# Router logits from extra columns, paired half-height products in the experts' first layer, and a GELU wait per chunk

## Chip, cores and metric

The kernel runs on one core of a Trainium2 chip. The metric is the device time of the program in microseconds (us). The engines are TensorE (PE in the profile; its weight loads are PEld), VectorE (DVE), ScalarE (ACT), GpSimd (POOL) and SyncE (SP, which here only issues DMAs).

## What is computed

The reference is one layer of a language-model tower on 32 sequences of 128 tokens with 192 features. Shortened to what matters here:

```python
emb  = word_table[ids] + domain_table[dom] @ proj_w.T + proj_b + types + pos
x    = layernorm(emb) * gamma + beta
x    = x + magnitude_attention(x)              # 12 heads of 16
x1   = plain_layernorm(x)                      # input of the transformer block
h    = x1 + causal_attention(ln1(x1)) @ proj_w + proj_b
z    = ln2(h)                                  # (h - mean) * rstd * ln2_w + ln2_b
logits = z @ w_g                               # 8 experts, router
sel  = top2(logits)                            # capacity 1280 rows an expert
hid  = gelu(z_rows @ fc_w[e] + fc_b[e])        # 192 -> 768
out  = hid @ pj_w[e] + pj_b[e]                 # 768 -> 192, added back with the router's weight
```

Everything is float32. Most large products are split by hand into fp32r parts (a high part and the low remainder), each of which TensorE multiplies in one pass. Products of plain float32 stand in the trace as two matmuls each.

## The kernel before, in words

**Attention.** Tokens are handled in 8 groups of 4 tiles (a tile is one sequence, 128 tokens on the partitions). The kernel makes passes of 16 slots. In a pass one group computes its scores while the group before it has its probabilities turned (`probT`), multiplied with the values, and its context written back. Groups 0 to 7 are the magnitude attention, groups 8 to 15 the causal attention. The order of work is written out by tables: `LAGS`, `LAST_LAGS` (for the last group), `CAU_PROJ`, `CAU_VALUE` and so on say in which slot each step of a tile is due, `causal_fills` and `fills_of` turn this into a list, and each item of that list (a fill) takes the next of three PSUM banks, `ps_ring`. TensorE, ScalarE and VectorE walk through the same list, each in its own order.

**The steps behind a causal tile.** `ctx` turns the context, VectorE divides it by the sums of the softmax into `ctx_n`; `ctxT` turns it again, ScalarE copies it to `ctxn_t` (L1095); `out` is the projection (L840 with 128 rows of contraction, L841 with the other 64). VectorE adds the bias (L1350) and the block's input (L1353), and takes the moments (L1356, L1358). GpSimd raises the variance to -1/2 (L577, L579). VectorE makes the normalised `z` (`normalise_z`, L1375). TensorE turns it (`zT`, two transposes on L761, ident,z), ScalarE copies it with the second layernorm's weight and bias to `z_t` (L1098, L1100), TensorE multiplies it with the gate (`logits`, L850 with 128 rows and L851 with 64), VectorE copies the logits (L1362) and takes the eight best and their places (L1364, L1366). GpSimd meanwhile adds `xin` to the residual (L712) and copies `z` into `xin` (L717), from where SyncE stores it as the row that the experts gather.

**Routing.** `route_tokens` on VectorE ranks the choices. It starts when the last tile's logits are ordered.

**Experts.** For each of 8 experts, 10 tiles of 128 rows come in three chunks of 2, 4 and 4 tiles (`CHUNKS`). TensorE works in this order: `first_layer` of a chunk, `turn_x` of the next chunk (transposes), `second_layer` of the chunk. `first_layer` makes 6 columns of 128 hidden features; each is five fp32r products (`split_product`, L769): high row part with high and low weights, low row part with high weights, and two products for the last 64 features, whose high part lies on partitions 0 to 63 and whose low part on 64 to 127 of `x_hi[:, 1]`. The six use three PSUM banks in turn; each waits until the GELU that read its bank is done (L1237, `gelus`). `second_layer` (L1016) waits for all GELUs of the chunk, then runs 6 float32 products a tile. `whole_x` on ScalarE (L1226) takes the turned rows out of PSUM, `split_x` on VectorE (L1692, L1694, L1695) splits them, two tiles at a time in one buffer `x_full`, so the two engines alternate. VectorE's `add_bias` (L1707, L1711) and GpSimd's indirect DMA (L643) finish a tile.

**Start.** TensorE, ScalarE and VectorE make small tables; VectorE waits for the split weights of the first attention (L1273, L1275), adds up the first gathered rows (L1474) and then starts the first group's embedding.

## Time and profile before

| What | Value |
|---|---|
| Median of 3 runs | 1075.64 us (1070.26 to 1076.09) |
| The profiled execution: its own time | 1077.97 us |
| Its span, first to last instruction | 1076.3 us |
| PE busy | 944.3 us, 88% |
| PEld busy | 723.7 us, 67% |
| ACT busy | 676.3 us, 63% |
| DVE busy | 666.5 us, 62% |
| POOL busy | 465.7 us, 43% |
| Mean granted TensorE clock | 0.92 |

The stages lie about as follows: tables and first gathers to 40 us, magnitude attention to 430, causal attention to 692, routing to 725, experts to the end. An average over the span mixes these, so the rows below are of single stages. A start and a duration in a timeline row are in us; matmuls overlap in the record, so what one costs is read from the distance between two starts, not from its duration.

### The profile page before, as it was taken

What the parts mean: (1) busy time and instruction counts of PE and PEld (TensorE: products, weight loads), DVE (VectorE), ACT (ScalarE), POOL (GpSimd) and SP (SyncE); (2) the same over time, 40 slices, a digit from 0 to 9 for tenths busy, and PEclk for the clock granted to TensorE, in tenths of its full rate; (3) what the DMA queues carried; (4) which work ended last, traced back from release to release, by engine and by line L of the source; (5) the groups of instructions that cost most, each with busy time, mean ns of one, the idle gap of its engine ahead of it and who ended that gap; (6) DMA issues with size and microseconds to landing.
All of it is one profiled execution on the core that took longest, in us unless ns stands there. A gap on an engine that the chain in (4) does not pass through costs nothing.

```text
span 1076.3 us, 22090 instructions
## 1 busy us (share of the span) xinstructions
PE 944.3 (88%) x7210; PEld 723.7 (67%) x7210; DVE 666.5 (62%) x3063; ACT 676.3 (63%) x1446; POOL 465.7 (43%) x508
## 2 busy tenths in 40 slices
PE   2487888999998799999999999567999999999996
PEld 1344655666665566767667766356988888888885
DVE  1576889988987767677767664673344343343332
ACT  2148789979888888778878886264344344344441
POOL 7677666740011001231231122205667666667654
PEclk7668899999999899999989996758999999999999
DMA  7333323321102000101101111226544346454342
GB/s 212 68 61 68 56 53 70 58 34 31 26 12 56 1 2 2 36 2 36 37 1 36 36 36 49 56 52 108 73 83 103 65 100 86 81 103 90 47 49 29
DMA packets 63364, 59.24 MB, mean 55 GB/s; under 512 B 17406, under 2 KB 54304, under 8 KB 63264
## 3 DMA queue, kind: packets, MB, share of 16 engines
q0 software_dynamic: 25344, 27.89, 18.4%
q1 hardware_dynamic: 37728, 29.85, 10.5%
q8 instruction: 51, 0.84, 0.3%
q14 instruction: 49, 0.40, 0.1%
q10 hardware_dynamic: 192, 0.26, 0.1%
HBM read 35.28 MB, written 16.39 MB: 48 GB/s over the span
## 4 chain that ended last, share of the span: by engine, by line
PE 60%; DVE 14%; SPq 7%; ACT 6%; issue 6%; POOL 4%; DMA 3%; POOLq 0%; DVEq 0%; ACTq 0%
PE ps_scores L769 13%; PE ps_ring L761 10%; PE ps_ring L1016 8%; SPq L494 6%; PE ps_ring L769 6%; PE ps_ctx L904 5%; PE ps_scores L1016 4%; PE ps_scores L890 4%; PE ps_scores L887 4%; POOL got L583 3%; DVE probs L1394 2%; DMA k<-k_signed 1%; PE ps_ring L841 1%; PE ps_ring L840 1%; DVE probs L1400 1%
## 5 line engine op out<-in xcount | busy, mean ns | idle before, releaser
L1237 ACT ACTIVATE probs<-ps_scores,fc_bias 128x512 f32<-128x512 f32 (+1 forms) x144 | 88.2, 616 | 148.2 <-PE ps_scores L769 144.7
L643 POOL DMA_INDIRECT out<-z_t,slots_now x80 | 135.4, 1693 | 103.4 <-DVE z_t L1711 84.5
L1105 ACT ACTIVATE prob_t<-ps_ring 128x512 f32<-128x512 f32 x192 | 114.1, 597 | 43.2 <-PE ps_ring L761 42.5
L761 PE MATMUL ps_ring<-ident,probs 128*128 128x128 f32 x768 | 127.9, 293 | 11.7 <-ACT q L1073 6.0
L1130 ACT ACTIVATE probs<-probs,neg_max 128x128 f32<-128x128 f32 x384 | 121.5, 397 | 4.7 <-DVE neg_max L1400 4.7
L1114 ACT ACTIVATE square<-ps_scores 128x512 f32<-128x512 f32 x192 | 104.5, 600 | 26.7 <-PE ps_scores L887 20.0
L1016 PE MATMUL ps_ring<-work,probs 128*128 128x192 f32 x672 | 115.9, 328 | 5.6 <-ACT probs L1237 5.4
L1400 DVE CUSTOM_DVE_ANT_0 probs<-ps_scores,causal 128x128 f32<-128x128 f32 x384 | 88.7, 287 | 50.6 <-PE ps_scores L890 50.4
L1016 PEld LDWEIGHTS ps_ring<-work,probs 128*128 128x128 f32 x672 | 109.2, 190 | 9.4 <-issue 9.4
L761 PEld LDWEIGHTS ps_ring<-ident,probs 128*128 128x128 f32 x768 | 91.9, 149 | 30.9 <-issue 11.0
L769 PE MATMUL ps_scores<-x_hi,fc_hi 128*128 128x512 f32 (+1 forms) x288 | 105.3, 371 | 7.4 <-DVE x_hi L1695 4.8
L1692 DVE CAST x_hi<-x_full 128x512 fp32r<-128x512 f32 x40 | 18.4, 459 | 138.1 <-ACT x_full L1226 138.1
L1394 DVE CUSTOM_DVE_ANT_0 probs<-square 128x128 f32<-128x128 f32 x384 | 89.1, 289 | 23.0 <-ACT square L1114 22.7
L769 PE MATMUL ps_scores<-x_hi,fc_lo 128*128 128x512 f32 (+1 forms) x288 | 102.0, 360 | 0.0
L887 PE MATMUL ps_scores<-k,q 32*128 32x256 f32 x768 | 89.1, 457 | 9.8 <-DMA k<-k_signed 6.9
L577 POOL TENSOR_SCALAR rstd<-z_moments 128x1 f32<-128x1 f32 x32 | 7.6, 238 | 182.4 <-DVE z_moments L1358 182.4
L577 POOL TENSOR_SCALAR rstd<-moments 128x4 f32<-128x4 f32 x24 | 7.0, 293 | 183.4 <-DVE moments L1525 115.4
L769 PE MATMUL ps_ring<-x_hi,w_hi 128*128 128x512 f32 x160 | 71.8, 448 | 7.3 <-DVE k L1316 3.3
L887 PEld LDWEIGHTS ps_scores<-k,q 32*128 32x128 f32 x768 | 44.3, 196 | 35.1 <-issue 13.0
L769 PEld LDWEIGHTS ps_scores<-x_hi,fc_hi 128*128 128x128 f32 x288 | 55.1, 191 | 18.7 <-issue 4.4
L769 PE MATMUL ps_ring<-x_hi,w_lo 128*128 128x512 f32 x160 | 65.3, 408 | 0.0
L761 PE MATMUL ps_ring<-ident,xn 128*128 128x128 f32 x160 | 29.8, 319 | 40.2 <-DVE xn L1461 30.5
(217 smaller groups left out, 2211.7 us busy)
## 6 DMA issues: line engine op xcount, KB each, us to landing
k<-k_signed SPq DMA_DIRECT2D x176, 32.0 KB
work<-pj_w SPq DMA_DIRECT2D x8, 576.0 KB, 4.3
token_in<-xin SPq DMA_DIRECT2D x8, 384.0 KB, 3.1
out<-resid SPq DMA_DIRECT2D x8, 384.0 KB, 4.1
vals<-fc_w SPq DMA_DIRECT2D x8, 384.0 KB, 3.3
vals<-fc_w SPq DMA_DIRECT2D x16, 192.0 KB, 4.0
out<-z_t,slots_now POOLq DMA_INDIRECT x80, 3.6
token_in<-xin SPq DMA_DIRECT2D x8, 128.0 KB, 4.2
```

Of the source, the lines that this page charges most:

```text
L494: sp.dma_start(k_of[g % 2][to:to + HEAD_DIM, b, 1, :, :].rearrange("p s k -> p (s k)"), k_signed[of:of + HEAD_DIM, b, :]).then_inc(keys_tu ...
L643: gp.indirect_dma_start(out[:, :], bass.IndirectOffsetOnAxis(slots_now[:, u, 1, t:t + 1], 0), slot_y[:, o, :], None, compute_op=ALU.add).t ...
L761: return pe.transpose(dst, src, ident[0:n, 0:n])
L769: last = pe.matmul(dst, lhs, rhs, start=(k == 0), stop=(k == 4))
L887: last = pe.matmul(ps_scores[:, h, 0:256], q[r, b, s, :], k[r, b, :, s, :], start=True, stop=True)
L1016: last = pe.matmul(ps_y[i][:, 0:HID], hidden[:, c % 2, f_, tok], pj_w_sb[:, u, f_, :], start=(f_ == 0), stop=(f_ == FF_CHUNKS - 1))
L1105: sc.activation(prob_t[:, s % 2, :, :], src.rearrange("p (h q) -> p h q", h=4), ACT.Exp if p is mag else ACT.Copy).then_inc(ring_free[i], 1)
L1114: sc.activation(square[:, j % 2, h, :, :].rearrange("p h m k -> p h (m k)"), ps_scores[:, h, 0:256], ACT.Square).then_inc(mag.scores_free, 1)
L1130: last = sc.activation(probs[:, j, h, :], probs[:, j, h, :], ACT.Exp, bias=neg_max[:, s, 4 * b + h:4 * b + h + 1], scale=-1.0)
L1237: sc.activation(hidden[:, c % 2, f_, 0:128 * nt], ps_scores[:, i, 0:128 * nt], ACT.Gelu, bias=fc_bias[:, e, f_:f_ + 1]).then_inc(gelu_done ...
L1394: last = ve.tensor_tensor_reduce(out=probs[:, j, h, :], in0=square[:, j % 2, h, 0, :], in1=square[:, j % 2, h, 1, :], scale=1.0, scalar=-3 ...
L1400: last = ve.tensor_tensor_reduce(out=probs[:, j, h, :], in0=ps_scores[:, h, 0:128], in1=causal[:, :], scale=-(HEAD_DIM ** -0.5), scalar=3. ...
```

## The change

1. The router's logits come as 8 more columns. `v_hi`, `v_lo`, `o_w`, `xin` are 200 wide (`WITH_GATE`). The columns are prepared once before the first pass (`gate_columns` on TensorE, `scale_gate` and `make_gate` on VectorE). The block's input gives its share of the logits through the causal value product, the attention through the output projection; the projection's bias is a 65th row of contraction against a column of ones in `ctx_n`. The fills `zT` and `logits`, ScalarE's two copies to `z_t`, VectorE's `normalise_z`, its copy of the logits and its separate add of the bias are gone. VectorE gains an add-on to each value fill, a small operation a tile (`order_experts`) and a reciprocal a group. GpSimd normalises into `xin` itself instead of copying.
2. In `first_layer` the fifth product of each hidden column uses only 64 rows. Two columns are handled as a pair: four products each, then their two last products on rows 0 to 63 and on rows 64 to 127. The second needs the high part on the lower partitions too: VectorE copies it to `x_rest`.
3. `second_layer` waits for each hidden column's GELU ahead of that column's first product, not for all ahead of the first.

```diff
-LAGS = {"ctx": 5, "ctxT": 7, "out": 9, "scale": 10, "norm": 12, "zT": 14, "keep": 14, "logits": 16}
-LAST_LAGS = {"ctx": 5, "ctxT": 6, "out": 8, "scale": 8, "norm": 10, "zT": 11, "keep": 11, "logits": 13}
+LAGS = {"ctx": 5, "ctxT": 7, "out": 9, "scale": 10, "norm": 12, "keep": 13}
+LAST_LAGS = {"ctx": 5, "ctxT": 6, "out": 8, "scale": 8, "norm": 10, "keep": 10}
...
-    for what in ("ctxT", "out", "zT", "logits"):
+    for what in ("ctxT", "out"):
...
+            load(o_w[REST:REST + 1, 1, 0:HID], rows[3:4, :])
             load(g_w[:, 0, :], gate_w[0:128, :])
             load(g_w[0:REST, 1, :], gate_w[128:HID, :])
+            load(g_w[REST:128, 1, :], gate_w[128:HID, :])
...
-                pool.wait_ge(z_ready, n + 1)
-                gp.tensor_copy(xin[:, n, :], z[:, s % 2, :]).then_inc(z_kept, 1)
+                pool.wait_ge(cau.named("z_rstd"), n + 1)
+                gp.tensor_scalar(xin[:, n, 0:HID], xin[:, n, 0:HID], z_moments[:, s % 2, 0:1], rstd[:, 4 + s % 2, 0:1],
+                                 ALU.subtract, ALU.mult).then_inc(z_kept, 1)
...
-                    last = transpose(dst[0:REST, 128:256], ctx_n[:, 128:HID])
+                    last = transpose(dst[0:REST + 1, 128:256], ctx_n[:, 128:HID + 1])
...
-                    pe.matmul(dst[:, 0:HID], ctxn_t[:, 0, :], o_w[:, 0, :], start=True, stop=False)
-                    last = pe.matmul(dst[:, 0:HID], ctxn_t[0:REST, 1, :], o_w[0:REST, 1, :],
-                                     start=False, stop=True)
-                elif kind == "zT":
-                    pe.wait_ge(z_ready, GROUP * g + s + 1)
-                    transpose(dst[:, 0:128], z[:, s % 2, 0:128])
-                    last = transpose(dst[0:REST, 128:256], z[:, s % 2, 128:HID])
-                elif kind == "logits":
-                    taken_out(number, ("zT", s))
-                    tok = slice(128 * s, 128 * s + 128)
-                    pe.matmul(dst[:, 0:EXPERTS], z_t[:, 0, tok], g_w[:, 0, :], start=True, stop=False)
-                    last = pe.matmul(dst[:, 0:EXPERTS], z_t[0:REST, 1, tok], g_w[0:REST, 1, :],
+                    pe.matmul(dst[:, 0:WITH_GATE], ctxn_t[:, 0, :], o_w[:, 0, :], start=True, stop=False)
+                    last = pe.matmul(dst[:, 0:WITH_GATE], ctxn_t[0:REST + 1, 1, :], o_w[0:REST + 1, 1, :],
                                      start=False, stop=True)
...
+            gate_columns()
             for p in PASSES:
...
+                for pair in range(FF_CHUNKS // 2):
+                    for f_ in (2 * pair, 2 * pair + 1):
+                        i = f_ % FC_RING
+
+                        pe.wait_ge(gelu_done[i], e * 6 + 2 * c + f_ // FC_RING + 1)
+                        first = pe.matmul(ps_scores[:, i, tok], fc_hi[:, u, 0, col(f_)], x_hi[:, 0, tok],
+                                          start=True, stop=False)
...
+                        for w, x in ((fc_lo[:, u, 0, col(f_)], x_hi[:, 0, tok]),
+                                     (fc_hi[:, u, 0, col(f_)], x_lo[:, tok]),
+                                     (fc_hi[:, u, 1, col(f_)], x_hi[:, 1, tok])):
+                            pe.matmul(ps_scores[:, i, tok], w, x, start=False, stop=False)
+                    for f_, rows_, x in ((2 * pair, top, x_hi[top, 1, tok]), (2 * pair + 1, bottom, x_rest[bottom, tok])):
+                        i = f_ % FC_RING
+                        pe.matmul(ps_scores[:, i, tok], fc_lo[rows_, u, 1, col(f_)], x,
+                                  start=False, stop=True).then_inc(fc_full[i], 1)
...
-                for i in range(FC_RING):
-
-                    pe.wait_ge(gelu_done[i], e * 6 + 2 * c + 3)
...
                     for f_ in range(FF_CHUNKS):
+                        if t == t0:
+
+                            pe.wait_ge(gelu_done[f_ % FC_RING], e * 6 + 2 * c + f_ // FC_RING + 2)
...
+                    dve.wait_ge(cau.named("unscaled"), g + 1)
+                    ve.tensor_scalar(xin[:, GROUP * g + s, HID:WITH_GATE], src[:, HID:WITH_GATE],
+                                     unscale[:, g % 2, s:s + 1], None, ALU.mult).then_inc(free, 1)
...
-                    ve.tensor_tensor(out_b, src[:, 0:HID], row_c[:, 3, :], ALU.add).then_inc(free, 1)
-
+                    ve.tensor_tensor(xin[:, t, :], xin[:, t, :], src[:, 0:WITH_GATE], ALU.add).then_inc(free, 1)
                     dve.wait_ge(free, n + 2)
-                    ve.tensor_tensor(xin[:, t, :], xin[:, t, :], out_b, ALU.add
-                                     ).then_inc(p.named("layer_sum"), 1)
...
+                dve.wait_ge(gate_turned, 1)
+                for c, n in ((0, 128), (1, REST)):
+                    some = slice(256 * c, 256 * c + 129 + REST)
+                    ve.tensor_copy(o_turned[0:n, some], ps_ring[0:n, 0, some]).then_inc(gate_made, 1)
+                dve.wait_ge(gate_turned, 2)
...
+                dve.wait_ge(gate_turned, 3)
+                for c, n in ((0, 128), (1, REST + 1)):
+                    ve.tensor_copy(o_w[0:n, c, HID:WITH_GATE], ps_ctx[0:n, 16 + 8 * c:24 + 8 * c]
+                                   ).then_inc(gate_made, 1)
...
                         ve.tensor_copy(x_hi[:, :, tok], x_full[:, :, :]).then_inc(ex_high, 1)
+                        ve.tensor_copy(x_rest[hl, tok], x_full[hl, 1, :])
                         dve.wait_ge(ex_high, e * (CAP_TILES // 2) + m + 1)
...
+            scale_gate()
             split_weights_low(mag_w_loaded, mag_w_high, mag_w_split, mag)
+            make_gate()
```

`gate_columns` is four float32 transposes and sixteen small float32 products on TensorE in three steps, each answered by VectorE. Between them `make_gate` also subtracts and copies blocks 8 columns wide.

```diff
+                for c in range(2):
+                    ve.scalar_tensor_tensor(out=gate[:, c, :], in0=ps_ctx[:, 0:EXPERTS], scalar=-1.0 / HID,
+                                            in1=gate[:, c, :], op0=ALU.mult, op1=ALU.add).then_inc(gate_made, 1)
...
+                ve.scalar_tensor_tensor(out=logits[:, s % 2, :], in0=xin[:, t, HID:WITH_GATE],
+                                        scalar=rstd[:, 4 + s % 2, 0:1], in1=gate_c[:, :], op0=ALU.mult, op1=ALU.add
+                                        ).then_inc(p.named("logits"), 1)
```

## Rows read from the trace of the kernel before

**Rows 1.** Stretches; columns: length, PE, PEld, DVE, ACT, POOL busy, PEclk, DMA share, GB/s.
```profile
200.00:300.00 100.00, 90.24 (x795) 60.49 (x794) 89.92 (x415) 85.66 (x151) 25.93 (x25) 1.00 0.19 38
...
514.00:551.00 37.00, 35.81 (x349) 25.91 (x348) 27.55 (x167) 30.59 (x84) 9.81 (x22) 1.00 0.09 27
...
557.00:563.00 6.00, 6.00 (x41) 4.01 (x39) 1.53 (x15) 3.89 (x10) 2.42 (x6) 0.51 0.00 0
...
850.00:900.00 50.00, 48.14 (x279) 43.84 (x278) 19.99 (x53) 19.52 (x33) 33.44 (x28) 1.00 0.49 87
```

**Rows 2.** Timeline of TensorE in a causal pass (start, duration, engine, line, operation).
```profile
542.95 0.39 PE L769 MATMUL ps_ring<-x_hi,w_hi 128*128 128x512 f32 x1
543.18 0.39 PE L769 MATMUL ps_ring<-x_hi,w_lo 128*128 128x512 f32 x1
543.50 0.82 PE L890 MATMUL ps_scores<-k,q 32*128 32x128 f32 x8
...
544.63 0.38 PE L761 MATMUL ps_ring<-ident,z 128*128 128x128 f32 x2
544.85 0.49 PE L840 MATMUL ps_ring<-o_w,work 128*128 128x192 f32 x2
545.27 0.59 PE L841 MATMUL ps_ring<-o_w,work 64*128 64x192 f32 x2
545.79 0.36 PE L769 MATMUL ps_ring<-v_hi,x_hi 128*128 128x192 f32 x1
545.99 0.27 PE L769 MATMUL ps_ring<-v_lo,x_hi 128*128 128x192 f32 x1
546.10 0.28 PE L769 MATMUL ps_ring<-v_hi,x_lo 128*128 128x192 f32 x1
...
547.57 0.39 PE L850 MATMUL ps_ring<-g_w,z_t 128*128 128x8 f32 x2 [0.32 <-DVE work L1329]
547.89 0.39 PE L851 MATMUL ps_ring<-g_w,z_t 64*128 64x8 f32 x2
548.21 0.66 PE L761 MATMUL ps_ring<-ident,probs 128*128 128x128 f32 x4
```

**Rows 3.** Groups by line and shape: ScalarE's first copy of a turned tile.
```profile
L1098 ACT ACTIVATE z_t<-ps_ring,ln_c 128x128 f32<-128x128 f32 x32 | 14.5, 453 | 12.4 <-PE ps_ring L761 11.5
```

**Rows 4.** Timeline of the end of the causal attention.
```profile
676.77 0.43 PE L904 MATMUL ps_ctx<-prob_t,work 128*32 128x128 f32 x8
...
679.93 0.48 ACT L1137 ACTIVATE ctx_t<-ps_ctx 128x384 f32<-128x384 f32 x1
...
688.34 0.64 DVE L1375 TENSOR_SCALAR z<-xin,z_moments,rstd 128x192 f32<-128x192 f32 x1 [1.00 <-POOL rstd L579]
...
691.26 0.59 PE L851 MATMUL ps_ring<-g_w,z_t 64*128 64x8 f32 x2
691.89 0.17 DVE L1362 COPY logits<-ps_ring 128x8 f32<-128x8 f32 x1 [2.37 <-PE ps_ring L851]
```

**Rows 5.** Timeline of the start, VectorE.
```profile
26.68 1.95 DVE L1474 TENSOR_TENSOR got<-got,square 128x768 f32<-128x768 f32 x2
```

**Rows 6.** Timeline of one expert's chunk of two tiles, to the next chunk's start.
```profile
902.51 1.28 ACT L1237 ACT_TABLE_LOAD   x1 [8.15 <-PE ps_scores L769]
...
904.33 0.39 PE L769 MATMUL ps_scores<-x_hi,fc_hi 128*128 128x256 f32 x1 [0.83 <-ACT probs L1237]
...
906.93 1.01 ACT L1226 ACTIVATE x_full<-ps_ctx,ln_c 128x256 f32<-128x256 f32 x2
...
911.29 0.42 DVE L1695 TENSOR_TENSOR x_hi<-x_full,x_hi 64x256 fp32r<-64x256 f32 x1
...
911.77 0.51 PE L769 MATMUL ps_scores<-x_hi,fc_hi 128*128 128x512 f32 x1 [0.33 <-DVE x_hi L1695]
```

**Rows 7.** Timeline of a third chunk: transposes, then the second layer.
```profile
767.09 0.60 PE L761 MATMUL ps_ring<-ident,xn 128*128 128x128 f32 x4
...
768.30 4.16 PE L1016 MATMUL ps_ring<-work,probs 128*128 128x192 f32 x24 [0.61 <-ACT probs L1237]
```

138 lines of the change are left out of this document (82 added, 56 removed).

## The prediction

> **What bounds the kernel now.** I read the stretches first, because an average over the span mixes three stages. In a causal pass of 37 us TensorE is busy 35.8, ScalarE 30.6, VectorE 27.6 [rows 1]: TensorE bounds it, with 1.2 us idle. In the experts it is busy 48.1 of 50 and ScalarE and VectorE 20 each [rows 1]. So what counts is where TensorE's starts move. The timelines of TensorE come second: there the distance from one start to the next is the cost, since recorded durations overlap.
>
> **Three prices on TensorE.** In steady state an fp32r product of 128x512 follows the last after 0.23 us (542.95 to 543.18), one of 192 columns after 0.11 [rows 2]. From 128-row products to 32-row ones the distance is 0.32 (543.18 to 543.50), 0.09 more [rows 2]. Where rows of contraction go from 128 to 64, two products of 192 columns take 0.42 and the next two 0.52 [rows 2]. If the 0.42 contains the same 0.09, two of them cost 0.33 without a change of height; the 0.52 then contains a second change and another 0.10, which I take for a weight load that could not be fetched early. The first value product after it shows that too: 0.20 to the next, against 0.11 [rows 2]. So a change of height costs **0.09**, and the first product after it **0.10** more. Against that, products on different rows do run side by side: the eight records of L890, on four row groups, end 0.82 after the first started although one record lasts some 0.3 or more [rows 2].
>
> The Trainium skill, page "TensorEngine Tiling (Array Packing)", section "Theoretical Speedup", gives up to 2x for contractions of at most 64 rows; by that alone a pair of last products would cost one slot and nothing else. The same page under "Tiling Modes" says that changing the tiling mode drains TensorE, and the trace agrees, with the 0.09 above. I let the measured price stand in the sum; the first sentence's outcome is a rival below.
>
> **Part 1, the router, in the causal passes.** Removed for each tile on TensorE: the two turns of z, 0.22 (544.63 to 544.85), and the four logits records, 0.64 (547.57 to 548.21) [rows 2]. The output projection changes height no more, if 65 rows count as 128: its second half falls from 0.52 to 0.33, its first half and the product after it lose 0.09 each, and eight more columns on two products add 0.03: 0.34 saved. The first product after the logits gains another 0.05. Together 1.25 us a tile. The value products stay at 0.11, since 200 columns are shorter than the distance that 192 already have to the weights' pace; if they grow with the columns it is 5 x 0.005, nothing. 28 of the 32 tiles lie in full passes: **35 us** as a ceiling. The other engines lose work too: ScalarE two copies of 0.45 a tile [rows 3], 3.6 a pass, so 27.0; VectorE one add of 0.36, one scaling of about 0.4 and a copy of 0.17, for two operations on eight columns of 0.17 [rows 4] and one reciprocal a pass, so about 25.5. With TensorE at 30.8 instead of 35.8 they stand at 0.85 and 0.8 of a 32 us pass. In the magnitude stage, where they are at 0.86 and 0.90, TensorE reaches 90 of 100 [rows 1]. So I take 85% of the ceiling, **-30 us**, with 21 (60%) and 38 (all of it and the 0.32 waits ahead of the logits, [rows 2]) as bounds. GpSimd's two-scalar operation in place of a copy hides: 9.8 of 37 busy [rows 1].
>
> **Part 1, the end of the stage.** For the last tile everything from z (688.34) to the logits' copy (691.89) is in series, 3.55 us [rows 4]. Ahead of it the last context copy on ScalarE starts at 679.93, though the values product that it reads ended at 677.20 (676.77 + 0.43) [rows 4]; queued before it are copies of z. That is 2.7 us. One add of 0.4 goes as well. Sum 6.6, taken as **-6.5**, from 3.5 (the queue finds another cause) to 8.
>
> **Part 1, the start.** `make_gate` stands on VectorE between the weights' split and the first rows' sum at 26.68 [rows 5], and everything behind it (moments, GpSimd's power, its later gathers) waits for VectorE. It is two copies of 193 columns (about 0.35 each), six or seven operations of about 0.17, and a wait for eight float32 records of TensorE, which at the start runs at half clock: two such records took from 691.26 to 691.89 with the copy's wake-up [rows 4], so four pairs at 0.5 to 0.6, some 2.2 us, of which 0.4 is covered. Sum 0.7 + 1.2 + 1.8 + wake-ups 0.4 = **+4 us**, between +1 (a slack behind it) and +6. The DMA that SyncE gains is ahead of waits that last longer.
>
> **Part 2, the pairs.** Of 10 slots of 0.23 one goes (-0.23); two changes of height (+0.18) and two uncovered weight loads (+0.20) come: **+0.15 us** a pair of 512 columns. For 256 columns the slot is half, 0.12, so +0.26. The two larger chunks of an expert have three pairs each: +0.9.
> The small chunk is worse, because its first GELU is late. ScalarE's table load (902.51, 1.28) and the GELU lead to TensorE's restart at 904.33 [rows 6]; they can begin only when the pair is finished, four products and the changes later: +0.7. The rest of the chunk is two pairs and a half, +0.55. Then two GELUs stand before the x copy at 906.93 instead of one, +0.4 [rows 6]. VectorE's `x_rest`, 64x256, lies between 0.17 (a tiny operation, [rows 4]) and 0.42 (a subtraction of this shape, [rows 6]); a copy has one input, so 0.25, twice in the chain that ScalarE and VectorE alternate on: +0.5. TensorE already waits for this chain at 911.77 [rows 6], so all of it counts: +2.2 us. In the other two chunks the second layer of four tiles (48 records at 4.16 us for 24, so 8 us, [rows 7]) covers it.
>
> **Part 3, the GELU waits.** In the third chunk TensorE goes from the transposes at 767.09 to the second layer at 768.30 [rows 7]; four transposes are 0.44, so 0.77 is wait. The second chunk has four transposes more, so about 0.33. Waiting per column, four columns (8 records of 4.16/24, 1.4 us) run first, and both late GELUs (0.7 each) fit beside transposes and these: -1.1 us an expert. In the small chunk the gain drowns in the chain of x. Sum for an expert: 0.9 + 2.2 - 1.1 = +2.0; eight: **+16 us**, from +10 (if the chunk's x chain has hidden slack) to +24 (x_rest 0.42, GELUs colliding).
>
> **Sum.** -30 - 6.5 + 4 + 16 = -16.5 us. The profiled execution took 1077.97; it would take 1061.5. The median of the runs is 2.3 us below the profiled one, so I forecast **1060 us**. About 0.5% (5.4 us) is what a measurement of this kernel can tell from no change.
>
> **Rivals.**
> *Free pairs.* By the rule of speedup quoted above the halves cost one slot and no drain. Then each pair saves 0.23 or 0.12, the larger chunks 1.4 an expert and part 3 1.1; the late first GELU and x_rest still cost about 1.3: -1.2, eight -10. Total -42.5: 1033. Against it: both places in rows 2 where the height changes to 64. Chance 0.14.
> *No side-by-side.* Two halves of 64 rows run one after the other. Each pair gets its slot back: 6 x 0.23 + 3 x 0.12 = 1.7 an expert, +14: 1074. Against it the 32-row products; but no row shows 64-row ones. Chance 0.12.
> *Another engine takes over in the causal passes.* ScalarE and VectorE, with three ring banks, hold the pass at about 35.5: only -10 there, 1080. For it: the magnitude stage [rows 1]. Against: in-order waits in the causal passes are near nil now. Chance 0.08.
> *Slower: the clock in the experts.* The granted clock is 1.00 there, but fell to 0.51, the level of 1.2 GHz, for 6 us while TensorE was busy with small products of the causal stage [rows 1]. With pairs TensorE idles some 1.5 us (0.83 and 0.7) inside each small chunk [rows 6] and about as long ahead of the next. If each of these brings one stretch at half clock, of 6 us, it costs 3 us an expert, 24 in all: 1084. It decides from 2.9 us an expert. Against it: idles of 0.8 at 904 did nothing [rows 1, 6]. Chance 0.06.
> That the kernel does not do what it says hardly can be: the only place is the 65-row product, if it kept the cost of 64; that is -0.34 x 28 = 9.5 less, within the forecast's range (1069).
>
> **Chances and range.** Forecast 0.60 (own range 1047 to 1071 from the bounds above), free pairs 0.14, no side-by-side 0.12, another engine 0.08, clock 0.06. Faster by over 0.5% means below 1070.3: 0.57 out of the forecast's 0.60, all of the free pairs and a third of the halves in turn: 0.75. Within: 0.03 + 0.08 + 0.06 = 0.17. Slower 0.08. To leave out no more than 2 in 10 the range takes in the free pairs and the halves in turn: 1034 to 1075.
>
> **What would show it.** Right: the causal pass about 32.5 us; L841 records with the same form as L840; from the last L769 of four to a 64-row one 0.32 and to the next 128-row one about 0.43; TensorE's restart in the small chunk 0.7 us later after the chunk's first product than now; L1016 no longer idle behind L1237; VectorE's first sum at about 30.7. Wrong: a distance of 0.23 across the height change (free pairs), 0.23 between the two halves (no side-by-side), a pass still over 35 us, or a granted clock well under 1.00 in the experts.

## The result and the profile after

The changed kernel takes 1070.48 us (median of 20 runs, 1064.9 to 1077.98 but for one of 1379.11, which the comparison leaves out) against 1076.82 for the kernel before (20 runs). The ratio is 0.9936, interval [0.991, 0.9962]: 0.64% faster, some 6.9 us, where 16.5 were forecast. The profiled execution took 1069.8 us.

The head of its page:

```profile
span 1068.0 us, 21602 instructions
PE 921.4 (86%) x7038; PEld 688.0 (64%) x7038; DVE 659.1 (62%) x3090; ACT 645.4 (60%) x1382; POOL 487.4 (46%) x509
```

TensorE is busy 23 us less and ScalarE 31 us less than before, and of that 8.3 us reached the span. I cut the span at four marks that both traces have: the first scores of the causal stage, the start of `route_tokens` (VectorE's `gap`), the first product of the first expert, the end.

| Stretch | Before | After | Difference | Forecast |
|---|---|---|---|---|
| To the first causal scores | 373.4 | 376.0 | +2.6 | +4 |
| Causal stage | 319.3 | 286.4 | -32.9 | -36.5 |
| Routing, to the first expert | 40.0 | 41.3 | +1.3 | 0 |
| Experts | 343.6 | 364.3 | +20.7 | +16 |

The first row is not resolved by one profile each: over all runs below the first causal scores start at 373.4 to 383.2 us without the router part and at 376.0 to 388.6 with it.

**Causal passes.** Stretches of before and after (columns as in [rows 1]): first a pass of before, its last one with the drain of the stage, and the experts.

```profile
478.70:515.80 37.10, 35.91 (x353) 25.95 (x352) 27.64 (x167) 30.70 (x84) 9.81 (x22) 1.00 0.10 27
...
628.00:692.70 64.70, 57.75 (x489) 39.15 (x488) 37.98 (x206) 40.91 (x109) 17.72 (x41) 0.81 0.17 49
...
740.00:1030.00 290.00, 279.82 (x1598) 253.15 (x1597) 118.54 (x315) 121.01 (x202) 188.37 (x148) 1.00 0.49 84
```

The same three after, and a pass at a lower clock:

```profile
475.50:509.10 33.60, 31.48 (x328) 23.20 (x328) 25.93 (x164) 27.87 (x76) 12.43 (x22) 1.00 0.11 29
509.10:545.40 36.30, 34.30 (x329) 25.05 (x328) 26.08 (x164) 27.99 (x76) 12.45 (x22) 0.91 0.10 27
...
613.50:662.40 48.90, 39.73 (x425) 27.51 (x424) 31.60 (x183) 33.12 (x89) 22.40 (x38) 0.93 0.21 55
...
740.00:1030.00 290.00, 274.83 (x1516) 227.05 (x1514) 113.16 (x327) 107.96 (x192) 183.96 (x148) 1.00 0.48 80
```

A pass at clock 1.00 falls from 37.1 to 33.6 us. TensorE's busy time falls by 4.43 us; the pass only by 3.5, because TensorE's idle time grew from 1.2 to 2.1. The last pass with the drain falls from 64.7 to 48.9. In the experts 290 us hold 82 matmuls fewer than before, at the same clock of 1.00, with TensorE less busy: it waits more.

The output projection is as forecast. TensorE's timeline after:

```profile
634.09 0.55 PE L768 MATMUL ps_ring<-ident,ctx_t 128*128 128x128 f32 x3
634.47 0.50 PE L849 MATMUL ps_ring<-o_w,work 128*128 128x200 f32 x2
634.81 0.51 PE L850 MATMUL ps_ring<-o_w,work 65*128 65x200 f32 x2
635.15 0.94 PE L768 MATMUL ps_ring<-ident,probs 128*128 128x128 f32 x4
```

With 65 rows of contraction the second half starts 0.34 after the first and costs 0.34, instead of 0.42 and 0.52 [rows 2].

**End of the stage and routing.** The timeline after, VectorE and GpSimd (POOL):

```profile
660.34 0.23 POOL L584 TENSOR_SCALAR rstd<-z_moments 128x1 f32<-128x1 f32 x1 [0.34 <-DVE z_moments L1392]
...
661.26 0.54 DVE L1398 SCALAR_TENSOR_TENSOR logits<-xin,rstd,gate_c 128x8 f32<-128x8 f32 x1 [1.00 <-POOL rstd L586]
...
661.88 1.07 POOL L723 TENSOR_SCALAR xin<-xin,z_moments,rstd 128x192 f32<-128x192 f32 x1
...
663.75 0.69 DVE L1662 TENSOR_TENSOR work<-work,choice 128x512 bf16<-128x512 f32 x1 [0.99 <-POOL spare_row L750]
```

From the start of the last power on GpSimd (raising the variance to -1/2) to the end of the logits it takes 1.5 us (660.34 to 661.80), without the chain from z to the logits' copy [rows 4]. But VectorE then waits 0.99 us in the routing for GpSimd's iota, which stands behind L723, the two-scalar operation of 1.0 us that took the place of a copy.

**Start.** VectorE's timeline after:

```profile
29.86 0.23 DVE L1481 COPY o_w<-ps_ctx 128x8 f32<-128x8 f32 x2 [1.43 <-PE ps_ctx L958]
30.02 1.94 DVE L1529 TENSOR_TENSOR got<-got,square 128x768 f32<-128x768 f32 x2
```

The sum that answers to [rows 5] is 3.3 us later, and the first scores of the first attention start at 59.77 instead of 54.80 (54.4 to 55.9 in the three kernels without the router part).

**Experts.** From one expert to the next TensorE took 42.02 us before and takes 44.71 (from the first expert's first product to the eighth's, divided by seven): +2.69 where the forecast had +2.0. The first expert alone takes 4.3 more (47.7 against 43.4), the next six 2.4 each; why the first differs comes below, under the clock. A pair of the larger chunks on TensorE:

```profile
898.67 0.40 PE L1036 MATMUL ps_scores<-x_hi,fc_hi 128*128 128x512 f32 x1
899.00 0.49 PE L1039 MATMUL ps_scores<-x_hi,fc_lo 64*128 64x512 f32 x1
899.00 0.49 PE L1039 MATMUL ps_scores<-w_hi,fc_lo 64*128 64x512 f32 x1
899.42 0.50 PE L1028 MATMUL ps_scores<-x_hi,fc_hi 128*128 128x512 f32 x1
899.76 0.39 PE L1036 MATMUL ps_scores<-x_hi,fc_lo 128*128 128x512 f32 x1
```

The two halves do start together. Yet it is 0.33 from the last full product to them, 0.42 back to 128 rows and 0.34 to the next: 1.09 in all. In the old order this stretch is four slots of 0.233, 0.93, so a pair loses 0.16. The small chunk and what follows, TensorE, ScalarE and VectorE:

```profile
885.20 0.39 PE L1039 MATMUL ps_scores<-w_hi,fc_lo 64*128 64x256 f32 x1
...
885.76 1.28 ACT L1270 ACT_TABLE_LOAD   x1 [7.50 <-PE ps_scores L1039]
...
887.58 0.39 PE L1028 MATMUL ps_scores<-x_hi,fc_hi 128*128 128x256 f32 x1 [1.32 <-ACT probs L1270]
...
891.35 1.02 ACT L1259 ACTIVATE x_full<-ps_ctx,ln_c 128x256 f32<-128x256 f32 x2
...
896.93 0.50 PE L1028 MATMUL ps_scores<-x_hi,fc_hi 128*128 128x512 f32 x1 [1.58 <-DVE x_hi L1752]
...
911.60 2.22 PE L1054 MATMUL ps_scores<-work,probs 128*128 128x192 f32 x12 [0.24 <-DVE z_t L1764]
...
921.53 1.79 PE L1054 MATMUL ps_ring<-work,probs 128*128 128x192 f32 x10
```

TensorE stops behind the first GELU until 887.58, and stops 1.58 us ahead of the next chunk where it stopped 0.33 before [rows 6]. The row at 911.60 is a wait that was not there: the second layer of the second chunk waits for VectorE to take out a bank. At 921.53 nothing waits for a GELU any more [rows 7].

### The profile page after: what moved, and what is told of

Same layout as the page of the kernel before. It is cut to its first block, busy times and chain, and to the rows that moved or that the text cites. A ratio compares the mean times of both kernels' runs of the same rounds, so it can differ in the third digit from the quotient of the medians.

```text
span 1068.0 us, 21602 instructions
## 1 busy us (share of the span) xinstructions
PE 921.4 (86%) x7038; PEld 688.0 (64%) x7038; DVE 659.1 (62%) x3090; ACT 645.4 (60%) x1382; POOL 487.4 (46%) x509
## 4 chain that ended last, share of the span: by engine, by line
PE 55%; DVE 18%; ACT 10%; issue 6%; SPq 5%; DMA 3%; POOL 2%; ACTq 0%; POOLq 0%; DVEq 0%
PE ps_ring L768 10%; PE ps_scores L1036 8%; PE ps_ring L776 7%; PE ps_scores L886 5%; PE ps_ring L1054 5%; PE ps_ctx L903 5%; SPq L500 4%; PE ps_scores L1028 4%; PE ps_scores L889 4%; PE ps_scores L1054 3%; PE ps_scores L1039 3%; ACT x_full L1259 2%; DVE probs L1428 2%; ACT square L1147 1%; ACT probs L1156 1%
## 5 line engine op out<-in xcount | busy, mean ns | idle before, releaser
L1270 ACT ACTIVATE probs<-ps_scores,fc_bias 128x512 f32<-128x512 f32 (+1 forms) x144 | 80.9, 613 | 172.6 <-PE ps_scores L1039 172.5
L768 PE MATMUL ps_ring<-ident,probs 128*128 128x128 f32 x768 | 124.5, 287 | 12.5 <-ACT q L1111 5.9
L1428 DVE CUSTOM_DVE_ANT_0 probs<-ps_scores,causal 128x128 f32<-128x128 f32 x384 | 88.7, 287 | 50.6 <-PE ps_scores L889 50.0
L1422 DVE CUSTOM_DVE_ANT_0 probs<-square 128x128 f32<-128x128 f32 x384 | 89.2, 288 | 23.6 <-ACT square L1147 20.7
L1028 PE MATMUL ps_scores<-x_hi,fc_hi 128*128 128x512 f32 (+1 forms) x144 | 62.5, 434 | 18.5 <-DVE x_hi L1752 11.4
L889 PE MATMUL ps_scores<-k,q 32*128 32x128 f32 x768 | 59.8, 326 | 12.5 <-DVE neg_max L1428 12.4
L886 PEld LDWEIGHTS ps_scores<-k,q 32*128 32x128 f32 x768 | 44.8, 198 | 30.8 <-issue 12.7
L1442 DVE TENSOR_TENSOR probs<-probs,row_root 128x512 f32<-128x512 f32 x96 | 63.2, 686 | 0.4
L889 PEld LDWEIGHTS ps_scores<-k,q 32*128 32x128 f32 x768 | 38.4, 186 | 34.1 <-DVE neg_max L1428 21.0
```

The source lines that it names most:

```text
L768: return pe.transpose(dst, src, ident[0:n, 0:n])
L886: last = pe.matmul(ps_scores[:, h, 0:256], q[r, b, s, :], k[r, b, :, s, :], start=True, stop=True)
L889: last = pe.matmul(ps_scores[:, h, 0:128], q[r, b, s, :], k[r, b // 2, 0, s, :], start=True, stop=True)
L1028: first = pe.matmul(ps_scores[:, i, tok], fc_hi[:, u, 0, col(f_)], x_hi[:, 0, tok], start=True, stop=False)
L1422: last = ve.tensor_tensor_reduce(out=probs[:, j, h, :], in0=square[:, j % 2, h, 0, :], in1=square[:, j % 2, h, 1, :], scale=1.0, scalar=-3 ...
L1428: last = ve.tensor_tensor_reduce(out=probs[:, j, h, :], in0=ps_scores[:, h, 0:128], in1=causal[:, :], scale=-(HEAD_DIM ** -0.5), scalar=3. ...
```

## Experiments

All ratios are to the kernel before, run beside each kernel on the same chip. "F, T, S" are the lengths on TensorE of a chunk's first layer, of the transposes behind it, and of its second layer up to the next chunk's first product; small is the chunk of two tiles, then second and third.

### The parts one by one

`r1_router` has part 1 alone, `r2_pairs` part 2 alone, `r3_gelu` part 3 alone, `r4_router_gelu` parts 1 and 3. As a diff of the changed kernel, `r4_router_gelu` is

```diff
-                for pair in range(FF_CHUNKS // 2):
...
-                    for f_, rows_, x in ((2 * pair, top, x_hi[top, 1, tok]), (2 * pair + 1, bottom, x_rest[bottom, tok])):
...
+                for f_ in range(FF_CHUNKS):
...
+                    split_product(ps_scores[:, i, tok], (x_hi[:, 0, tok], x_lo[:, tok], x_hi[:, 1, tok]),
...
-                        ve.tensor_copy(x_rest[hl, tok], x_full[hl, 1, :])
```

and `r1_router` moves the three waits of the second layer back ahead of its first product as well:

```diff
+                for i in range(FC_RING):
+                    pe.wait_ge(gelu_done[i], e * 6 + 2 * c + 3)
...
-                        if t == t0:
-                            pe.wait_ge(gelu_done[f_ % FC_RING], e * 6 + 2 * c + f_ // FC_RING + 2)
```

`r3_gelu` is the reverse of that on the kernel before; `r2_pairs` is the first diff reversed on it. Part 3 waits per hidden column; the wait per chunk that the title names is that of the kernel before.

> Part 1 alone (router's columns), first and second layer of the experts as before. Theory A (the three parts have the sizes that the two traces show, and only the experts' terms were mis-sized): routing starts at about 662 us as in the changed kernel, experts at 42.0 us each as before, so 30 to 33 us less than before minus up to 1.5 for the routing stage: ratio 0.970 to 0.974. Rival B (the router's gain itself is small and most of what it saves comes back behind it): ratio 0.985 or more.

> Part 2 alone (paired last products and x_rest), router and GELU waits as before. Theory A: the pairs are a loss, 0.15 us for each of six pairs of 512 columns, about 2.4 in the small chunk, an expert 3 to 3.5 us longer: 24 to 28 us slower, ratio 1.022 to 1.026. Rival B (pairs nearly neutral): within 8 us of before.

> Part 3 alone (a wait for each column's GELU). Theory A: 1.1 us an expert at most (0.33 in the second chunk, 0.77 in the third), 6 to 9 us faster, ratio 0.992 to 0.994. Rival B (VectorE's late release of the second layer's banks gives the second chunk's part back even without the pairs): 5 to 6 us, and TensorE idle behind L1711 in the second layer of the second chunk.

> Parts 1 and 3, without the pairs and x_rest. Theory A: the sum of the two, 36 to 41 us faster than before, ratio 0.962 to 0.967, about 1037 us, and 26 to 33 us faster than the whole change. Rival B: under 20 us faster than before.

| Kernel | Median us | Ratio | Interval | One expert |
|---|---|---|---|---|
| r1_router | 1055.8 | 0.9757 | [0.9724, 0.9789] | 42.0 |
| r2_pairs | 1115.08 | 1.0314 | [1.0281, 1.0347] | 46.5 |
| r3_gelu | 1070.24 | 0.9894 | [0.9872, 0.9915] | 40.83 |
| r4_router_gelu | 1043.78 | 0.9653 | [0.9625, 0.968] | 40.83 |

The router saves 2.4% (26 us), the GELU waits 1.1% (11 us; 1.19 x 8 = 9.5 in the trace), and the pairs alone cost 3.1% (34 us). Without the pairs the change is worth 3.5%. The pairs take 2.8% back: 0.9936 against 0.9653, or 44.71 - 40.83 = 3.88 us an expert, 31 in all. So the large gain of the router is real and is spent in the experts. Only `r4_router_gelu` lies within what was expected of it. `r1_router` is a little above 0.974, `r2_pairs` well above 1.026, and `r3_gelu` below 0.992; its rival B falls, since its second chunk's second layer takes 7.67 us, with no wait for VectorE. Where the 3.88 lie:

| | small F | T | S | second F | T | S | third F | T | S |
|---|---|---|---|---|---|---|---|---|---|
| r4_router_gelu | 3.64 | 0.87 | 4.76 | 7.10 | 0.87 | 7.67 | 7.13 | 0.44 | 7.67 |
| after | 5.06 | 0.93 | 5.51 | 7.49 | 0.93 | 8.18 | 7.52 | 0.49 | 7.67 |

(These are single experts behind the first, whose differences add up to 3.6 us; small F is that without the table load of GELU, with it 4.75 and 6.30. The first expert is 5.1 longer and lifts the mean to 3.88.) In `r2_pairs`, where the second layer still waits for all GELUs, both GELUs of a pair come after the last product. TensorE's timeline there, for the second and third chunk:

```profile
1033.95 2.19 PE L1027 MATMUL ps_scores<-work,probs 128*128 128x192 f32 x12 [0.62 <-ACT probs L1248]
...
1050.95 4.14 PE L1027 MATMUL ps_ring<-work,probs 128*128 128x192 f32 x24 [1.05 <-ACT probs L1248]
```

Its T is 1.71 and 1.70 us where the kernel before has 1.23 and 1.21. That is 0.97 us an expert, where the T beside part 3 grow by 0.11; against it S of the second chunk stays at 7.74 there. So the pairs alone cost more than the pairs beside part 3.

### Order or height

`e5_order` is `r4_router_gelu` with the order of the pairs (four, four, then the two last products), but these on all 128 rows, and without `x_rest`:

```diff
+                    for f_ in (2 * pair, 2 * pair + 1):
+                        i = f_ % FC_RING
+                        pe.matmul(ps_scores[:, i, tok], fc_lo[:, u, 1, col(f_)], x_hi[:, 1, tok],
+                                  start=False, stop=True).then_inc(fc_full[i], 1)
```

`e6_half_alone` keeps the order of before and makes the fifth product 64 rows high:

```diff
-                                   fc_lo[:, u, 1, col]), False,
+                                                (fc_lo[0:REST, u, 1, col], x_hi[0:REST, 1, tok]))):
```

> Router and GELU waits of the change; first layer in the order of the pairs (four, four, one, one) but with all products at full height and no x_rest. It isolates the order. Theory A (order, height change and x_rest each cost): the larger chunks' first layer stays at 7.1 us, the small chunk is 0.8 to 1.3 us longer because its first GELU comes later: 7 to 10 us slower than the same kernel without pairs (ratio to before about 0.972 to 0.975). Rival B (the height change is all of the loss): within 2 us of it, ratio 0.965 to 0.967.

> Router and GELU waits of the change; first layer in the old order, but the fifth product of every column has 64 rows, with no partner beside it. It leaves nothing out of the result, and measures two changes of height a column: 144 columns by 0.38 us is 55 us if the two changes (0.09 each) and the two uncovered weight loads (0.10 each) count in full; 45 to 55 us slower than the same kernel at full height, ratio to before 1.007 to 1.017. If a height change costs nothing when a product stands alone: ratio 0.965.

`e5_order`: 1047.13 us, 0.9747 [0.9695, 0.9798], 42.05 an expert: the order costs 1.21 an expert, 9.7 us, all in the small chunk (F 4.49, S 5.04; the others as in `r4_router_gelu`). Its timeline shows how, inside the second pair:

```profile
998.20 0.28 PE L1034 MATMUL ps_scores<-x_hi,fc_hi 128*128 128x256 f32 x1
998.54 0.38 PE L1026 MATMUL ps_scores<-x_hi,fc_hi 128*128 128x256 f32 x1
```

The fourth column of the chunk (998.54) needs the bank of the first, whose GELU started only behind the first pair. It starts 0.34 behind the product ahead of it, where steady products of 256 columns start 0.12 apart.

`e6_half_alone`: 1095.4 us, 1.0157 [1.0085, 1.0229], 47.57 an expert, +6.74 for 18 half products. Its timeline gives the prices one by one:

```profile
1053.07 0.40 PE L1028 MATMUL ps_scores<-x_hi,fc_hi 128*128 128x512 f32 x1
1053.39 0.50 PE L1028 MATMUL ps_scores<-x_hi,fc_lo 64*128 64x512 f32 x1
1053.82 0.50 PE L1028 MATMUL ps_scores<-x_hi,fc_hi 128*128 128x512 f32 x1
1054.16 0.39 PE L1028 MATMUL ps_scores<-x_hi,fc_lo 128*128 128x512 f32 x1
```

0.32, 0.43, 0.34 and then 0.22 again. Against 0.23 each that is 0.09 + 0.20 + 0.11 = 0.40 for a visit to the other height and back. This holds whether one product or two stand there; in the changed kernel the second one is free and gives 0.23 back. A pair loses 0.16 us, and the rule of the Trainium skill, page "TensorEngine Tiling (Array Packing)", section "Tiling Modes", that a change of mode drains TensorE, agrees with these rows.

### The small chunk and the copy

`e7_small_old` is the changed kernel with the small chunk in its old form and no `x_rest` for it; `e8_xrest_twice` is the changed kernel with the copy made twice:

```diff
+                if c == 0:
+                    for f_ in range(FF_CHUNKS):
...
+                    return
...
+                        if c > 0:
+                            ve.tensor_copy(x_rest[hl, tok], x_full[hl, 1, :])
```

```diff
                         ve.tensor_copy(x_rest[hl, tok], x_full[hl, 1, :])
+                        ve.tensor_copy(x_spare[hl, tok], x_full[hl, 1, :])
```

> The whole change, but the small chunk of each expert in the old form and without its x_rest. Theory A (of the pairs' 31 us about 18 lie in the small chunk and the second layer behind it, 13 in the larger ones): ratio to before 0.974 to 0.979. Rival B (the larger chunks carry most of it): 0.985 or more. The second layer of the second chunk keeps its wait behind VectorE (8.2 us instead of 7.7).

> The whole change with VectorE's x_rest copy (0.29 us) made twice. Theory A (it lies in the chain that ScalarE and VectorE alternate on, twice ahead of the second chunk's first layer and twice ahead of VectorE's release of the second layer's banks): 1.1 us an expert, 8 to 9 us slower than the change, ratio to before about 1.001. Theory A2 (only the first of these counts): 0.6 an expert, 5 us, 0.998. Rival B (hidden): 0.9936 as the change.

`e7_small_old`: 1057.24 us, 0.9812 [0.9758, 0.9866]. The ratio can't decide between what was expected and its rival; the length of an expert can: 42.8, so 1.9 of the pairs' 3.88 us, about half, are the small chunk's own pairs (F 3.64 again, the rest in S). What stays against `r4_router_gelu`: S of the small chunk +0.54 (there the next chunk's rows are split, with two copies), second F and third F +0.39 each, the transposes +0.06 and +0.05, and S of the second chunk +0.51.

`e8_xrest_twice`: 1083.31 us, 1.0052 [1.0023, 1.0082], 46.24 an expert, +1.53. That is more than was expected, and not all of it is the copy. S of the small chunk grows by 0.5 to 0.6, and S of the second chunk from 8.18 to mostly 8.59: 0.8 to 1.0 in four of the seven experts compared. The other three (the second, third and fifth) grow by 2.3 to 2.5, because there the granted clock fell to 1.2 GHz for 3.5 us, and the second chunk's F took 8.95 to 8.99 instead of 7.49:

```profile
768.30:771.80 3.50, 3.50 (x10) 2.01 (x8) 2.88 (x7) 0.00 (x0) 2.32 (x1) 0.51 0.17 19
```

TensorE had stood idle for 1.99 us just before (until 767.83). In the fourth expert the same idle was 1.95 us, and the clock stayed at 1.00. That the longer idles bring these falls was not tested by itself; the changed kernel's idles there are 1.3 to 1.6 us, with no fall. The second layer's wait grows with the copy:

```profile
1057.90 1.41 PE L1055 MATMUL ps_scores<-work,probs 128*128 128x192 f32 x7 [0.71 <-DVE z_t L1766]
```

Here it is 0.71 where the row at 911.60 has 0.24. This shows what that row is: VectorE splits four tiles of the next chunk's rows, now with two copies, before it comes to `add_bias`, and TensorE needs the bank that `add_bias` frees.

### What holds the causal pass at 33.6

`e10_dve_more` is `r4_router_gelu` with the statistics of each causal tile taken twice on VectorE, `e11_act_more` with the turned context copied twice on ScalarE, each time into a spare place:

```diff
+                    ve.bn_stats(z_spare[:, :], xin[:, t, 0:HID])
```

```diff
+                    sc.activation(work[:, 2304:2560].rearrange("p (c t) -> p c t", c=2),
+                                  src[:, 0:256].rearrange("p (c t) -> p c t", c=2), ACT.Copy)
```

> The same without pairs, with VectorE's moments of each causal tile (0.36 us) taken twice, the second into a spare tile. Theory A (VectorE's order sets the remaining idle of TensorE in a causal pass): the pass of 33.6 us grows by 0.7 to 1.4. Rival B (TensorE alone bounds it): by less than 0.2.

> The same without pairs, with ScalarE's copy of the turned context (0.38 us a causal tile) made twice. Theory A: ScalarE, 27.9 busy of 33.6, has slack, the pass grows by less than 0.3 us. Rival C (ScalarE is the new bound of the pass): by 0.8 to 1.5 us.

`e10_dve_more`: 1043.52 us, 0.9696 [0.9651, 0.974]; `e11_act_more`: 1044.45 us, 0.9698 [0.9652, 0.9745]. The ratios can't tell them from `r4_router_gelu`; the lengths of the passes can. Lengths in us from one group's first scores to the next's; the last goes to the start of the routing:

| Kernel | 1 | 2 | 3 | 4 | 5 | 6 | 7 | last |
|---|---|---|---|---|---|---|---|---|
| before | 31.8 | 34.5 | 38.9 | 37.1 | 37.1 | 39.9 | 35.2 | 64.6 |
| r3_gelu | 33.3 | 34.6 | 38.9 | 37.1 | 37.1 | 38.6 | 35.3 | 61.6 |
| after | 33.3 | 32.6 | 33.6 | 33.6 | 36.3 | 34.9 | 33.3 | 48.9 |
| r4_router_gelu | 32.2 | 32.6 | 36.1 | 34.8 | 34.9 | 36.2 | 33.3 | 47.7 |
| e10_dve_more | 32.2 | 33.1 | 34.4 | 34.4 | 34.4 | 35.6 | 33.6 | 50.6 |
| e11_act_more | 32.6 | 32.6 | 36.2 | 34.8 | 34.9 | 36.3 | 33.3 | 49.1 |

`e11_act_more` has the passes of `r4_router_gelu`: ScalarE has slack. In `e10_dve_more` a pass at clock 1.00 takes 34.4 instead of 33.6:

```profile
477.00:511.40 34.40, 31.52 (x329) 23.20 (x328) 26.82 (x168) 27.92 (x76) 12.44 (x22) 1.00 0.11 28
```

Four operations were added, VectorE's busy time grew by 0.9 us (25.93 to 26.82), and 0.8 of it lengthens the pass, though VectorE is busy only 0.78 of it. So it is not VectorE's amount of work that holds the pass, but its order. The waits of two passes say where (engine and line, what it waited for, us in total, times, longest), first of `r1_router`, then of the kernel before:

```profile
PEld ps_scores L888 <- DVE neg_max L1417: 5.5, 8, 1.7
...
PE ps_scores L888 <- DVE neg_max L1417: 3.5, 4, 1.5
```

```profile
PEld ps_scores L890 <- DVE neg_max L1400: 3.0, 8, 0.8
...
PE ps_scores L890 <- DVE neg_max L1400: 1.2, 2, 0.6
```

The scores' weight loads waited 3.0 us for `neg_max` in two passes before, and 5.5 in `r1_router`; the matmuls themselves waited 1.2 before and 3.5 then. That is 1.15 more a pass on the matmuls, enough for the 0.9 by which TensorE's idle time grew.

### The start and the routing

`e9_gate_in_waits` is `r4_router_gelu` with `make_gate` cut in two and put where VectorE waits for GpSimd during the first rows' normalisation. `e12_count_early` is that with GpSimd's iotas for the routing ahead of the last tile's keep:

```diff
+                        if g == 0 and at == 4:
+                            make_gate()
+                        if g == 0 and at == 10:
+                            finish_gate()
...
-            make_gate()
```

```diff
+                                if (n, due("keep", at, n)) == (2 * GROUPS - 1, GROUP - 1):
+                                    count_rows()
                                 keep_z(n - GROUPS, due("keep", at, n))
```

> Router and GELU waits without pairs (1043.8 us, ratio 0.9653), with make_gate cut in two and put behind VectorE's moments of the first group, where it waits 1.6 us for GpSimd each time. Theory A (the 3.3 us at the start pass on to the end): VectorE's first sum back at 26.7, the first scores 2 to 3 us earlier, ratio about 0.963. Rival B (the start has slack behind it, or the spread of the clock in the magnitude stage hides it): no difference, 0.965.

> The router and the GELU waits without the pairs and with make_gate cut in two, as in e9, and GpSimd's three iotas moved from behind the last tile's keep to ahead of it. Theory (the routing is 1.0 us longer than before because VectorE's first 512-wide operation waits for the iotas, which stand behind GpSimd's two-scalar operation of the last tile): that wait of 1.00 us is gone, from gap to the first expert's first product it takes 40.0 us instead of 41.0, and the ratio is about 0.1% under that of e9 (0.964), which a measurement can't tell. Rival (the routing is longer for another reason, such as the later stores of xin that the gathers wait for): the wait goes, and the distance stays at 41 us or grows, since the last tile's normalised rows now come 0.8 us later.

`e9_gate_in_waits`: 1038.07 us, 0.9652 [0.9614, 0.969]. Its VectorE:

```profile
26.67 1.94 DVE L1520 TENSOR_TENSOR got<-got,square 128x768 f32<-128x768 f32 x2
```

The first sum is back where it was, and the first scores start at 56.13 instead of 59.23 in `r4_router_gelu`. The ratio doesn't resolve these 3 us.

`e12_count_early`: 1041.25 us, 0.9632 [0.9589, 0.9674], profiled span 1037.6. GpSimd and VectorE there:

```profile
663.28 0.23 DVE L1391 SCALAR_TENSOR_TENSOR logits<-xin,rstd,gate_c 128x8 f32<-128x8 f32 x1 [1.00 <-POOL rstd L585]
...
663.89 0.60 POOL L718 TENSOR_TENSOR resid<-resid,xin 128x192 f32<-128x192 f32 x1
664.11 0.46 DVE L1656 TENSOR_TENSOR gap<-work 128x32 f32<-128x32 f32 x1
...
664.60 1.55 POOL L722 TENSOR_SCALAR xin<-xin,z_moments,rstd 128x192 f32<-128x192 f32 x1
664.73 0.69 DVE L1661 TENSOR_TENSOR work<-work,choice 128x512 bf16<-128x512 f32 x1
```

The wait at `work,choice` is gone. From the last tile's power on GpSimd (662.71 and 662.67) to the first expert's first product it is 42.77 us in `e9_gate_in_waits` and 41.75 here: 1.0 less, as the theory had it, though the last tile's rows are stored later. From `gap` it is 40.3 instead of 41.0, because `gap` itself came 0.3 earlier behind that power (the logits' operation took 0.23 instead of 0.54). So of the wait of 1.00 only 0.7 came through from `gap` on, less than the 1.0 expected; `gap` took 0.25 longer. Of all kernels run it has the shortest span and the lowest ratio; by the ratio it can't be told from `r4_router_gelu` and `e9_gate_in_waits`, but it is 3% below the changed kernel (0.9632 against 0.9936).

## Why the prediction was right or wrong

The side was right and the size was not: -16.5 us forecast, -6.9 by ratio. The median, 1070.5, lies within the range and well above 1060. The profiled execution, 1069.8, answers to the 1061.5 of the sum.

**The three prices: right in size, one reading was not.** 0.32 to 0.33 into the 64-row product, 0.42 to 0.43 out of it, 0.34 for the next, two halves together in one slot. A pair cost 0.16 (2.49 from 899.42 to the same place of the next, against ten of 0.233), forecast 0.15. *Free pairs* and *No side-by-side* both fell on these rows: the distance is not 0.23, and the halves start within 0.01. But the second sign that the prediction gave for the 0.10, the first value product's 0.20 to the next, is none. It stands in the trace of before also where no height of 64 rows is near:

```profile
485.63 0.55 PE L761 MATMUL ps_ring<-ident,ctx_t 128*128 128x128 f32 x3
486.01 0.36 PE L769 MATMUL ps_ring<-v_hi,x_hi 128*128 128x192 f32 x1
486.21 0.27 PE L769 MATMUL ps_ring<-v_lo,x_hi 128*128 128x192 f32 x1
```

The 0.10 held by the other sign, the 0.52, and `e6_half_alone` measured 0.11.

**Part 1, the passes: the step that failed most.** "85% of the ceiling, -30 us" for 28 tiles is 4.3 a pass. The measured saving at clock 1.00 is 3.5 in passes 4 and 5, 1.9 in pass 2, 3.2 in pass 7 (35.2 to 32.0 in `e12_count_early`, both at 1.00). Over passes 1 to 7 the kernels without the router part take 254.3 us on average (before, `r2_pairs`, `r3_gelu`), the ten with it (all but `e10_dve_more`) 238.2: -16, where six sevenths of the forecast are -26. Two terms of the sum were off, and one was not in it. TensorE lost 4.43 us a pass, not 5.0. And the allowance for other engines, 15%, was too small: of 4.43 only 3.5 came through, because the scores wait for `neg_max` behind VectorE's list. The rival *Another engine takes over* named the place and had it too strong (35.5 a pass); `e10_dve_more` shows VectorE, `e11_act_more` excludes ScalarE. What was not in the sum is the clock. Passes 2 to 7 take 221.5 us in `r2_pairs` and `r3_gelu`, with a mean granted clock of 0.985. With the router part they take 200.5 in the two runs at 0.99 (`e5_order`, `e12_count_early`), 204.1 in the changed kernel at 0.97 and 207.9 in the four at 0.94. At like clock the router part is worth 21 us there; the lower clock of most of these runs takes up to 7 of it back. Whether the router part causes the lower clock was not tested.

**Part 1, the end: more than forecast, and by luck.** The last pass with the drain takes 62.6 us on average without the router part and 48.5 with it: -14, where one seventh of the passes and the 6.5 make -10.8. But the term of 2.7 us in the 6.5 was misread. The last context copy on ScalarE waits for the last of three value products, and [rows 4] has an earlier one. The last one in the kernel before, then it and the copy after:

```profile
678.82 0.42 PE L904 MATMUL ps_ctx<-prob_t,work 128*32 128x128 f32 x8
```

```profile
652.84 0.43 PE L903 MATMUL ps_ctx<-prob_t,work 128*32 128x128 f32 x8
...
653.95 0.48 ACT L1170 ACTIVATE ctx_t<-ps_ctx 128x384 f32<-128x384 f32 x1
```

The copy at 679.93 came 0.69 behind its product, and after the change, with the copies of z gone, it still comes 0.68 behind: the term is nothing. The chain of z and the add were right: from this copy to `gap` it is 12.8 us without the router part and 8.5 with it, -4.3 where 3.95 were forecast. The rest, -9.8 (49.9 to 40.1 us), lies ahead of the copy, where a pass's share of 4.3 was forecast. A part of this is clock: up to the copy it is 0.84 to 0.90 without the router part and 0.92 to 1.00 with it. The nearest two, `r2_pairs` at 0.90 and `e6_half_alone` at 0.92, still differ by 7.2 (48.9 and 41.8). Why that is more than in a full pass was not tested, nor what makes the clock so. Together the causal stage gave 30 us on average of 36.5 forecast (32.9 in the two profiles of before and after).

**Part 1, the start: right at the place forecast.** 3.3 us at VectorE's first sum (forecast 4.0), and 5.0 at the first scores, 4.4 in `r4_router_gelu`. `e9_gate_in_waits` gets 3.1 of it back at the first scores. No run shows how much of it reaches the end.

**Part 1, the routing: missed.** The forecast wrote of GpSimd's new operation that it hides, since GpSimd is busy 9.8 of 37 us [rows 1]. In the passes it does. Behind the last tile nothing covers it, and the iotas that VectorE waits for stand in the same queue: +1.0 us from `gap` on. `e12_count_early` removes the wait of 1.00 and gets 0.7 of it back; that the last 0.3 is `gap`'s own 0.25, held up by another GpSimd operation, is read from its rows.

**Part 2, the small chunk: right in sum.** Forecast +2.2: late GELU 0.7, rest of the chunk 0.55, second GELU 0.4, `x_rest` 0.5. Measured: F +1.42 to +1.55 for the first two, T +0.06, S +0.75 for the others, of which `e7_small_old` gives 0.54 to the copies and `e5_order` 0.3 to the order. Sum 2.3. F was forecast at 1.25 and S at 0.9, so two misses of 0.2 cancel.

**Part 2, the larger chunks: a term was missing.** +0.9 forecast, +1.4 measured. The pairs are 0.39 in each chunk and the transposes behind a half 0.11, together the 0.9. The other 0.5 is the step "the second layer of four tiles covers it". It covers the chain of x, but not VectorE's `add_bias` behind that chain, and TensorE waits for `add_bias` in the second chunk. 8 x 0.5 = 4 us.

**Part 3: right.** -1.1 forecast, -1.19 measured an expert.

**Clock in the experts: a small part of that rival came.** From 740 us on it is 1.00 over 290 us, before and after. But the first expert lies ahead of that, and starts at 1.2 GHz in every kernel. Ten microseconds from its first product, before and after:

```profile
732.70:742.70 10.00, 9.96 (x58) 9.55 (x59) 1.95 (x7) 6.15 (x12) 3.24 (x5) 0.79 0.88 122
```

```profile
703.70:713.70 10.00, 9.13 (x36) 7.49 (x37) 0.49 (x3) 3.80 (x7) 3.07 (x5) 0.50 0.86 123
```

The low clock lasts about 3.5 to 5.2 us in the kernels whose small chunk has the old form, 8.5 in `e5_order`, 10.0 in the changed kernel and `e8_xrest_twice`, 12.2 in `r2_pairs` and 13.8 in `e6_half_alone`. So it goes with the order and the half products of the small chunk. By the first expert's 4.3 us against the 2.4 of the others it costs some 1.9 us, an estimate. Later falls of 3.5 us, as the rival had them, stand in the profiles of `e8_xrest_twice` (three) and `r2_pairs` (one), and in that of the changed kernel there are none.

Put together by differences of the profiles: 3.6 us short in the causal stage, 4.7 in the experts (2.3 in the first, 2.5 in the next six together, 0.2 less in the last), 1.3 in the routing, 1.4 better at the start: 8.2 of the forecast 16.5 are missing in the span. By the ratio 9.6 are missing. The passes vary from run to run with the granted clock (33.6, 34.8 or 36.3 for the same pass at 1.00, 0.95 and 0.91), so the third digit of such a balance is not to be trusted.

## What to carry to other kernels

Before two short products are put side by side, price the way there and back: here a visit to another height cost 0.40 us and a shared slot of 512 columns gave back 0.23, so that the pairing lost even though both halves ran at once. Work taken off the bounding engine comes through only as far as the next engine's order of work lets it: 4.4 us off TensorE made a pass 3.5 shorter, with VectorE busy at 0.77. A context copy that starts late is to be held against the last product that it waits for, not against the one that a view happens to show. An operation that hides in the middle of a stage needs a second look at its last instance, where it stands ahead of the next stage in its queue. And what hides a copy must be followed to everything behind it on its engine, not only to the one that reads it.

## What was not expected of the hardware

A GpSimd and a VectorE operation held each other up. The logits' operation of VectorE takes 0.22 or 0.23 us inside a pass, but 0.54 for the last tiles, where it starts 0.07 behind GpSimd's add L719 (0.59 long; L718 in the variants) and ends with it; in `e12_count_early` an iota stands in that place, and it takes 0.23 again. There `gap` meets the add and takes 0.46 instead of 0.21, and GpSimd's L722 takes 1.55 instead of 1.02 beside VectorE's operations. The Trainium skill, page "SBUF — State Buffer", section "SBUF: two separate sides", has it that a VectorE operation with two SBUF inputs and a GpSimd operation that reads SBUF share a port pair, and that whichever starts first holds it for its whole instruction. The logits' operation and `gap`, which have two inputs each and end with the add, agree with that. L722 does not by its recorded start: it is recorded 0.13 ahead of the 512-wide `work,choice`, which still takes its usual 0.69, and L722 is the one that takes longer; GpSimd's recorded times are rough. The sum of it is some 0.3 us on the path here.

Contraction over 65 rows was as fast as over 128, with no change of height around it: 0.34 instead of 0.52 for a product of 64 rows. An unneeded 65th row can be cheaper than stopping at 64.

A saving of busy time on TensorE did not always show as time, because the granted clock differed: identical passes of identical code took 33.6 us at 1.00 and 36.3 at 0.91. Over passes 2 to 7 it is 200.5 to 207.9 us among the kernels with the router part, 0.7% of the whole time, a large part of the runs' spread of about 1%. TensorE's busy share was the same, 0.94, in the pass at 1.00 and in the one at 0.91.

In the experts of `e8_xrest_twice` the granted clock fell to 1.2 GHz for 3.5 us behind idles of TensorE of 1.90, 1.99 and 2.18 us, and not behind one of 1.95.
